# Attention with 8-wide heads: the band mask of the first layer added after the scores, in two 64x64 blocks instead of whole tiles

## The chip, the cores and the metric

The kernel is one program on one core of a Trainium2 chip. The metric is the device time of that program in microseconds (us), from launch to end. PE is TensorE (matmuls), PEld its weight loads, DVE VectorE, ACT ScalarE, POOL GpSimd.

## The reference

Four layers of cross attention and feed-forward on 32 sequences of 128 tokens with 128 features. The change touches only the first attention: 16 heads, each 8 wide, and a band mask that hides key k from query q where |q - k| is over 64.

```
q = _heads(query @ Wq.T + bq)
k = _heads(key @ Wk.T + bk)
v = _heads(value @ Wv.T + bv)
scores = jnp.einsum('bhqd,bhkd->bhqk', q, k) / np.sqrt(D_HEAD).astype(np.float32)
idx = jnp.arange(S)
local = jnp.abs(idx[:, None] - idx[None, :]) <= WINDOW // 2      # WINDOW = 128
scores = jnp.where(local[None, None, :, :], scores, -jnp.inf)
attn = jax.nn.softmax(scores, axis=-1)
```

With 128 queries and 128 keys, the mask hides something only where query and key lie in different halves of 64: in the two 64x64 blocks off the diagonal. In the two on the diagonal it is zero everywhere.

## The kernel before

`small_heads(l, phase)` computes this attention for layer 0 (and, with another mask, for layer 2). It handles one sequence per iteration, n = 0 to 31, in groups g of four (j = n % 4). Scores are computed twice. The first time they are written as queries x keys into `S` (the PSUM tile `pair`, two banks of 512 columns, so 8 heads at once: two passes p = 0 and 1 for the 16 heads); DVE takes the maximum over keys of each head (`maximum`, line 768). `split_max` (lines 776, 778) makes two bf16 parts of the negated maxima, and PE turns them over with one transpose (`turn_max`, line 582, into the PSUM tile `single`). The second time the scores are computed as keys x queries into `T` (the PSUM tile `quad`, four banks, all 16 heads: `turned`, line 598), the turned maxima are added to them (line 604), ACT takes the exponential (line 748), and `attend` (line 621) multiplies by the values and by ones. DVE divides (`normalise`, lines 784 and 786).

The mask is added by PE too. `mask_banks` (line 156) multiplies a 64x64 piece of an identity (bf16) by a broadcast of the mask: four matmuls of 64x64 by 512 columns fill two banks. They start the accumulation (`start=True`), and the scores are added on top. `S` takes four of them per pass (`mask_scores`), `T` takes eight (`mask_turned`).

There is one `S`, so pass 1 is written only after DVE has read pass 0, which `mask_scores` waits for (`s_free`). Each engine runs its instructions in the order of the code. On PE the order of iteration n is written out by hand:

```
(j==0: project_q, j==1: project_v, j==2: output, j==3: turn)   # "the head of the iteration"
mask_turned(n)
mask_scores(n + 2, 0)
turn_max(n + 1)
turned(n)
scores(n + 2, 0)
attend(n - 1)
(j==3: project_k)
mask_scores(n + 2, 1)
scores(n + 2, 1)
```

On DVE it is: other work of the group, `maximum(n+2, 0)`, `normalise(n-1)`, `maximum(n+2, 1)`, `split_max(n+2)`. Ahead of the loop a warm-up runs `mask_scores`, `scores` and `maximum` four times (m = 0, 1 and p = 0, 1), and `turn_max(0)`.

Of the kernel before, what the change touches and what calls it, by code (L numbers as in the profile page):

```python
# [20 lines left out]
P = 128  # L21
# [52 lines left out]
def program(nc, t, out):  # L74
    ctx = ExitStack()
    with ctx:
        def sb(name, shape, dtype=F32):
            return ctx.enter_context(nc.sbuf_tensor(name, shape, dtype))

        def sem(name):  # L80
# [8 lines left out]
        identb = sb("identb", [P, P], BF16)  # L89
# [3 lines left out]
        mask_bias = {l: {n: [sb(f"mask{n}{l}{half}", [P, P], BF16)[:] for half in ("own", "other")] for n in names}  # L93
                     for l, names in ((0, "S"), (2, "ST"), (3, "S"))}
# [56 lines left out]
        def mask_banks(pe, banks, masks):  # L151

            for r in range(2):
                rows = slice(64 * r, 64 * r + 64)
                for c in range(2):
                    pe.matmul(banks[r][64 * c:64 * c + 64, :], identb[rows, rows],
                              masks[r ^ c][rows, :].unsqueeze(1).broadcast_to([64, 4, P]), start=True, stop=False,
                              skip_group_check=True)

        def loop(eng, group, groups=NG, done=0):  # L160

            with eng.Fori(done // 2, groups // 2 - 1) as i:
                for u in range(2):
                    group(2 * i + u, u, False)
            for u in range(2):
                group(groups - 2 + u, u, u == 1)
# [253 lines left out]
        def small_heads(l, phase):  # L420
# [8 lines left out]
            qT = [arena.take([W]) for _ in range(2)]  # L429
# [20 lines left out]
            S, T, O, M = pair, quad, bank[6], bank[7]  # L450
# [9 lines left out]
            def strip(r):  # L460
                return slice(32 * r, 32 * r + 32)
# [27 lines left out]
            def tensor(pe):  # L489
# [68 lines left out]
                def mask_scores(m, p):  # L558

                    pe.wait_ge(s["s_free"], 2 * m + p)  # L560
                    mask_banks(pe, [S[:, r * 512:(r + 1) * 512] for r in range(2)], mask_bias[l]["S"])

                def scores(m, p):
                    g, j = divmod(m, G)
                    if j == 0 and p == 0:
                        pe.wait_ge(s["q_evac"], g + 1)
                        pe.wait_ge(s["kv_ready"], g + 1)
                    for r in range(2):
                        rows = strip(2 * p + r)
                        mm = pe.matmul(S[:, r * 512:(r + 1) * 512], qT[g % 2][rows, j * P:(j + 1) * P],  # L570
                                       kv[g % 2][rows, j, :, :].rearrange("p a k -> p (a k)"),
                                       start=False, stop=True, skip_group_check=True)
                    mm.then_inc(s["s_ready"], 1)

                def turn_max(m):
# [8 lines left out]
                def mask_turned(n):  # L584
                    if n == 0:
                        pe.wait_ge(s["k_evac"], 2)
                        pe.wait_ge(s["q_evac"], 1)
                        pe.wait_ge(s["v_evac"], 1)
                    pe.wait_ge(s["st_free"], 2 * n)
                    for r in (0, 2):  # L590
                        mask_banks(pe, [T[:, i * 512:(i + 1) * 512] for i in (r, r + 1)], mask_bias[l]["T"])

                def turned(n):

                    g, j = divmod(n, G)
                    for a in range(4):
                        for r in range(4):
                            pe.matmul(T[:, r * 512 + a * P:r * 512 + (a + 1) * P], kv[g % 2][strip(r), j, a, :],  # L598
                                      qT[g % 2][strip(r), j * P:(j + 1) * P], start=False, stop=False,
                                      skip_group_check=True)  # L600
                    pe.wait_ge(s["mts_ready"], n + 1)
                    for a in range(4):
                        for r in range(4):
                            mm = pe.matmul(T[:, r * 512 + a * P:r * 512 + (a + 1) * P], chooser[strip(r), a, :],  # L604
                                           mts[n % 2][strip(r), :], start=False, stop=True, skip_group_check=True)
                    mm.then_inc(s["st_ready"], 1)

                def attend(m):
# [24 lines left out]
                mm = pe.matmul(O[:, 0:P], vcol, wo[:], start=True, stop=True)  # L633
                if l == 2:
                    pe.wait_ge(s["tables_ready"], 1)
                    pe.wait_ge(s["c_squared"], 1)
                    mm = pe.matmul(lg_part[:, 0:E], ones, cT2, start=True, stop=True)
# [8 lines left out]
                for m in range(2):  # L646
                    for p in range(2):
                        mask_scores(m, p)
                        scores(m, p)
                pe.wait_ge(s["cvec_ready"], 1)  # L650
                turn_max(0)
                for n in range(N):
                    g, j = divmod(n, G)
                    if j == 0 and routes(g):
                        turn_rows(g - 2)
                    if j == 0 and g + 1 < NG and l == 0:
                        project_q(g + 1, M)
                    elif j == 1 and g + 1 < NG:
                        project_v(g + 1, M)
                    elif j == 2 and g >= 1:  # L660
                        output(g - 1)
                    elif j == 3 and g + 2 < NG:
                        turn(g + 2)
                    mask_turned(n)
                    if n + 2 < N:
                        mask_scores(n + 2, 0)
                    if n + 1 < N:
                        turn_max(n + 1)
                    if j == 0 and g + 1 < NG and l == 2:
                        project_q(g + 1, M)  # L670
                    turned(n)
                    if n + 2 < N:
                        scores(n + 2, 0)
                    if n >= 1:
                        attend(n - 1)
                    if j == 3 and g + 2 < NG:
                        project_k(g + 2, M)
                    if n + 2 < N:
                        mask_scores(n + 2, 1)
                        scores(n + 2, 1)  # L680
# [1670 lines left out]
        def wide_heads(phase):  # L2351
# [131 lines left out]
            def tensor(pe):  # L2483
# [23 lines left out]
                def scores(t):  # L2507

                    g, j, o = t // 8, t // 2 % G, t % 2
                    if t % 8 == 0:  # L2510
                        ring_copied(pe, ("q", g, HB - 1))
                        ring_copied(pe, ("k", g, HB - 1))
                    if t >= 2:
                        pe.wait_ge(s["exp_done"], t - 1)
                    mask_banks(pe, [S[o][:, r * 512:(r + 1) * 512] for r in range(2)], mask_bias[3]["S"])
                    for i in range(4):
                        for r in range(2):
                            rows = slice(64 * r, 64 * r + 64)
                            mm = pe.matmul(S[o][:, r * 512 + i * P:r * 512 + (i + 1) * P],  # L2519
                                           qT[g % 2][rows, 4 * o + i, j * P:(j + 1) * P],  # L2520
                                           kT[g % 2][rows, 4 * o + i, j * P:(j + 1) * P],
                                           start=False, stop=(i == 3), skip_group_check=True)
                    mm.then_inc(s["s_ready"], 1)
# [365 lines left out]
```

## Time and profile before

| | before |
|---|---|
| device time, median of 3 runs | 2033.67 us (2032.84 to 2035.79) |
| span of the profiled execution, first to last instruction | 2027.5 us |
| first-layer attention loop within it | about 36.9 to 280 us |
| PE busy over the whole span | 1766.7 us (87%) |
| DVE busy over the whole span | 1092.1 us (54%) |
| ACT busy over the whole span | 891.5 us (44%) |

For the profiled execution the profile gives its span; its time with launch and end is not listed apart. The median of the runs is 6.2 us above the span, and that difference is taken as the work around the span. A row of the timeline gives the start in us from the span's start and the length. Matmuls overlap: the end of a PE row is modelled and lies behind the start of the next, so what PE really spends is read from start to start. The `f32` matmuls show twice as many instances in the trace as in the code, since each runs as two passes.

### The profile page before, as it was taken

How to read it: one execution, taken by the hardware profiler on the slowest of the kernel's cores; microseconds unless marked ns; L12 is line 12 of the kernel's file. 1: busy time of each engine (PE TensorE's matmuls, PEld its weight loads, DVE VectorE, ACT ScalarE, POOL GpSimd, SP SyncE). 2: the span in 40 equal slices, each digit the busy share in tenths (PEclk: the TensorE clock that was granted, in tenths of full speed). 3: DMA queues.
4: the chain of work that ended last, by engine and by line, in shares of the span. 5: the costliest groups of instructions: out<-in, count | busy, mean ns of one | idle time of the engine just before them, and what ended most of it. 6: DMA issues, size and time to landing. Idle time of an engine off the chain costs nothing.

```text
span 2027.5 us, 48497 instructions
## 1 busy us (share of the span) xinstructions
PE 1766.7 (87%) x18886; PEld 1258.1 (62%) x18886; DVE 1092.1 (54%) x3147; ACT 891.5 (44%) x2432; POOL 652.9 (32%) x656
## 2 busy tenths in 40 slices
PE   6999985587869999998999971999699999999978
PEld 3565564576648778873565551999456666666753
DVE  4666657567532222214566763656465656665548
ACT  2333320476334444432333320666265555556525
POOL 3233201467311111103214426455133233333405
PEclk8999996788679999997999995999799999999969
DMA  5000000000000000007210001222200000000001
GB/s 174 7 13 8 2 2 9 28 16 1 1 6 1 1 2 2 1 1 293 104 76 18 18 18 45 61 57 58 90 17 17 17 17 17 6 1 1 1 1 42
DMA packets 48828, 63.55 MB, mean 31 GB/s; under 512 B 8106, under 2 KB 37701, under 8 KB 48349
## 3 DMA queue, kind: packets, MB, share of 16 engines
q1 hardware_dynamic: 44253, 51.98, 7.8%
q0 software_dynamic: 4352, 8.47, 1.3%
q8 instruction: 156, 2.56, 0.5%
q14 instruction: 67, 0.55, 0.1%
HBM read 32.29 MB, written 28.65 MB: 30 GB/s over the span
## 4 chain that ended last, share of the span: by engine, by line
PE 57%; DVE 9%; issue 7%; POOL 4%; POOLq 3%; DVEq 2%; ACT 1%; DMA 1%; SPq 1%; PEldq 0%; PEld 0%; ACTq 0%
PE single L1835 5%; PE quad L1823 5%; PE pair L570 3%; PE single L621 3%; PE single L2156 3%; PE quad L2139 2%; PE quad L2145 2%; PE pair L1796 2%; PE quad L598 2%; PE pair L2519 2%; POOL tokens_by_expert L417 2%; DVE arena L768 1%; PE quad L2554 1%; PE quad L2545 1%; PE single L2531 1%
## 5 line engine op out<-in xcount | busy, mean ns | idle before, releaser
L768 DVE TENSOR_REDUCE arena<-pair 128x8 f32<-128x1024 f32 x128 | 156.7, 1224 | 140.4 <-PE pair L570 138.4
L2757 POOL TENSOR_TENSOR arena<-arena 128x512 f32<-128x512 f32 x128 | 130.4, 1040 | 296.2 <-DVE arena L2676 296.2
L263 POOL TENSOR_TENSOR rstd<-var_eps,neg_half 128x4 f32<-128x4 f32 (+1 forms) x64 | 65.5, 1024 | 350.3 <-DVE var_eps L259 266.7
L748 ACT ACTIVATE arena<-quad 128x1024 f32<-128x1024 f32 x128 | 124.1, 1021 | 69.3 <-PE quad L604 65.0
L1908 ACT ACTIVATE arena<-quad,arena 128x256 f32<-128x256 f32 x256 | 110.7, 475 | 98.1 <-PE quad L1823 98.1
L892 POOL TENSOR_SCALAR arena<-arena 128x512 f32<-128x512 f32 x56 | 86.7, 1565 | 196.6 <-ACT arena L690 196.5
L570 PE MATMUL pair<-arena 32*128 32x512 f32 x512 | 147.3, 652 | 0.0
L1999 DVE TENSOR_TENSOR arena<-single,arena 128x512 f32<-128x512 f32 x32 | 22.1, 692 | 206.2 <-PE single L1835 206.2
L2612 ACT ACTIVATE arena<-pair,arena 128x128 f32<-128x128 f32 x256 | 90.9, 381 | 89.0 <-DVE arena L2671 89.0
L2612 ACT ACTIVATE arena<-quad,arena 128x128 f32<-128x128 f32 x256 | 90.9, 381 | 86.4 <-DVE arena L2671 86.4
L1835 PE MATMUL single<-wide,arena 128*64 128x128 f32 x2048 | 123.9, 275 | 0.0
L1823 PE MATMUL quad<-arena,wide 128*128 128x256 f32 x512 | 121.6, 385 | 2.6 <-issue 1.8
L1835 PEld LDWEIGHTS single<-wide,arena 128*64 128x64 f32 x2048 | 110.7, 137 | 15.7 <-issue 10.0
L1823 PEld LDWEIGHTS quad<-arena,wide 128*128 128x128 f32 x512 | 93.2, 190 | 18.5 <-issue 6.4
L2336 POOL DMA_INDIRECT outputs_by_choice<-arena x72 | 71.0, 986 | 88.3 <-DVE arena L2289 72.9
L2280 DVE SCALAR_TENSOR_TENSOR arena<-quad,arena 114x128 f32<-114x128 f32 x216 | 62.4, 344 | 48.6 <-ACT arena L2190 25.1
L2190 ACT ACTIVATE arena<-quad,arena 114x128 f32<-114x128 f32 x216 | 63.5, 365 | 55.9 <-PE quad L2139 46.8
L784 DVE RECIPROCAL arena<-single 128x128 f32<-128x128 f32 x64 | 61.2, 957 | 47.8 <-PE single L621 37.3
L417 POOL DMA_INDIRECT tokens_by_expert<-arena x64 | 62.8, 981 | 74.8 <-PE single L621 37.8
L717 ACT ACTIVATE arena<-single 128x128 bf16<-128x128 bf16 x64 | 17.7, 277 | 151.4 <-PE single L582 151.0
L621 PEld LDWEIGHTS single<-arena 128*32 128x32 f32 x2048 | 52.3, 109 | 49.2 <-issue 48.8
L2033 POOL TENSOR_TENSOR arena<-arena 128x512 f32<-128x512 f32 x32 | 34.8, 1096 | 134.2 <-DVE arena L1978 134.2
(502 smaller groups left out, 4376.7 us busy)
## 6 DMA issues: line engine op xcount, KB each, us to landing
tokens_by_expert<-arena SPq DMA_DIRECT2D x22, 780.0 KB, 8.6
arena<-in_ctxT SPq DMA_DIRECT2D x32, 256.0 KB, 3.0
arena<-tokens_by_expert SPq DMA_DIRECT2D x72, 65.0 KB, 1.8
wide<-in_w SPq DMA_DIRECT2D x2, 2048.0 KB, 10.1
arena<-outputs_by_choice SPq DMA_DIRECT2D x16, 256.0 KB, 4.1
wide<-in_wgu SPq DMA_DIRECT2D x1, 2736.0 KB
x<-in_x SPq DMA_DIRECT2D x4, 512.0 KB, 7.9
out_x<-x SPq DMA_DIRECT2D x8, 256.0 KB, 2.3
```

The lines of the kernel that those rows point to most:

```text
L417: pool.indirect_dma_start(by_tile, bass.IndirectOffsetOnAxis(ap=where_i[:, i, n:n + 1], axis=0), xr[:, n, :], None).then_inc(routed, 16)
L570: mm = pe.matmul(S[:, r * 512:(r + 1) * 512], qT[g % 2][rows, j * P:(j + 1) * P], kv[g % 2][rows, j, :, :].rearrange("p a k -> p (a k)"), ...
L621: mm = pe.matmul(O[strip(c), k * P:(k + 1) * P], lhs(h), probs[m % 2][:, h, :], start=(a == 0), stop=(a == 3), skip_group_check=True)
L748: act.activation(probs[n % 2][:, 8 * p:8 * p + 8, :].rearrange("p h q -> p (h q)"), T[:, 1024 * p:1024 * p + 1024], ACT.Exp).then_inc(s["s ...
L768: dve.tensor_reduce(mx[m % 2][:, 8 * p:8 * p + 8], S[:].rearrange("p (h k) -> p h k", h=8), AX.X, ALU.max).then_inc(s["s_free"], 1)
L892: mm = pool.tensor_scalar(kv[g % 2][:, :, a, :], kf[g % 2], kmask[:, a:a + 1], None, ALU.mult)
L1823: pe.matmul(bank[2 + f][:, 0:G * K], w1[:, e, f * P:(f + 1) * P], exT[u][:, e, :], start=True, stop=True).then_inc(s["h_ready"], 1)
L1835: mm = pe.matmul(bank[6 + pair % 2][K * r:K * r + K, j * P:(j + 1) * P], h1T[e % 4][:, f, j * K:(j + 1) * K], w2[:, e, f, :], start=(f == ...
L1908: act.activation(h1T[e % 4][:, f, :], bank[2 + f][:, 0:G * K], ACT.Gelu_apprx_tanh, bias=b1c[:, e, f:f + 1]).then_inc(s["h_evac"], 1)
L2336: pool.indirect_dma_start(done, bass.IndirectOffsetOnAxis(ap=back_i[:, n:n + 1], axis=0), ysb[n % SLOTS], None, bounds_check=2 * B * P - 1 ...
L2612: mm = act.activation(probs[t % 3][:, i, :], S[t % 2][:, i * P:(i + 1) * P], ACT.Exp, bias=minus_max[t % 3][:, i:i + 1], accum_out=total[t ...
L2757: pool.tensor_tensor(part, part, inv[t % 3][:, 4 * r:4 * r + 4].unsqueeze(2).broadcast_to([P, 4, P]), ALU.mult).then_inc(s["norm_ready"], 1)
```

## The change

In layer 0 alone, `mask_banks` is not called any more. A new helper, `mask_across`, adds the mask only where it is not zero: each of its four matmuls writes 4 x 64 columns (in each of the four heads of a bank, the half of the columns that lies off the diagonal) instead of 512. It runs after the scores, as the end of the accumulation: behind the two score matmuls of each pass into `S`, and behind the added maxima in `T`. The first score matmul of each bank now starts the accumulation. The semaphores that tell DVE (`s_ready`) and ACT (`st_ready`) that a tile is ready are raised by the last mask matmul. The waits for a free tile stay where they were. Layer 2 keeps the code of before.

```diff
+        def mask_across(pe, banks, masks):
+
+            for r in range(2):
+                rows = slice(64 * r, 64 * r + 64)
+                for c in range(2):
+                    far = slice(64 - 64 * c, 128 - 64 * c)
+                    mm = pe.matmul(banks[r].rearrange("p (a k) -> p a k", a=4)[64 * c:64 * c + 64, :, far],
+                                   identb[rows, rows], masks[r ^ c][rows, far].unsqueeze(1).broadcast_to([64, 4, 64]),
+                                   start=False, stop=True, skip_group_check=True)
+            return mm
...
                 def mask_scores(m, p):
 
                     pe.wait_ge(s["s_free"], 2 * m + p)
-                    mask_banks(pe, [S[:, r * 512:(r + 1) * 512] for r in range(2)], mask_bias[l]["S"])
+                    if l == 2:
+                        mask_banks(pe, [S[:, r * 512:(r + 1) * 512] for r in range(2)], mask_bias[l]["S"])
...
-                                       start=False, stop=True, skip_group_check=True)
+                                       start=(l == 0), stop=True, skip_group_check=True)
+                    if l == 0:
+                        mm = mask_across(pe, [S[:, r * 512:(r + 1) * 512] for r in range(2)], mask_bias[l]["S"])
                     mm.then_inc(s["s_ready"], 1)
...
                     pe.wait_ge(s["st_free"], 2 * n)
-                    for r in (0, 2):
-                        mask_banks(pe, [T[:, i * 512:(i + 1) * 512] for i in (r, r + 1)], mask_bias[l]["T"])
+                    if l == 2:
+                        for r in (0, 2):
+                            mask_banks(pe, [T[:, i * 512:(i + 1) * 512] for i in (r, r + 1)], mask_bias[l]["T"])
...
-                                      qT[g % 2][strip(r), j * P:(j + 1) * P], start=False, stop=False,
+                                      qT[g % 2][strip(r), j * P:(j + 1) * P], start=(l == 0 and a == 0), stop=False,
...
+                    if l == 0:
+                        for r in (0, 2):
+                            mm = mask_across(pe, [T[:, i * 512:(i + 1) * 512] for i in (r, r + 1)], mask_bias[l]["T"])
                     mm.then_inc(s["st_ready"], 1)
```

Lines move by 11 to 18 with it: 570 becomes 582, 582 becomes 596, 598 and 604 become 613 and 619, 621 becomes 639, and the mask matmuls of layer 0 are at line 166. Two places on PE show what moves. The first is the middle of a loop iteration. Before, from the added maxima (line 604) over pass 0 of the scores (570) and `attend` (621) to pass 1 of the scores:

```order
L604 MATMUL quad<-arena 128x128 x16
L570 MATMUL pair<-arena 128x512 x2
L621 MATMUL single<-arena 32x128 x16
L621 MATMUL single<-arena,ones_cols 32x128 x16
L156 MATMUL pair<-maskS0own,identb 64x512
L156 MATMUL pair<-maskS0other,identb 64x512 x2
L156 MATMUL pair<-maskS0own,identb 64x512
L570 MATMUL pair<-arena 128x512 x2
```

And now, from the added maxima (619) over pass 0 of the scores (582) to `attend` (639):

```order
L619 MATMUL quad<-arena 128x128 x16
L166 MATMUL quad<-maskS0own,identb 64x4x64
L166 MATMUL quad<-maskS0other,identb 64x4x64 x2
L166 MATMUL quad<-maskS0own,identb 64x4x64 x2
L166 MATMUL quad<-maskS0other,identb 64x4x64 x2
L166 MATMUL quad<-maskS0own,identb 64x4x64
L582 MATMUL pair<-arena 128x512 x2
L166 MATMUL pair<-maskS0own,identb 64x4x64
L166 MATMUL pair<-maskS0other,identb 64x4x64 x2
L166 MATMUL pair<-maskS0own,identb 64x4x64
L639 MATMUL single<-arena 32x128 x16
L639 MATMUL single<-arena,ones_cols 32x128 x16
```

Twelve mask matmuls of half the columns have come in between the added maxima and `attend`; the four full ones between `attend` and pass 1 of the scores are gone.

The second place is the end of an iteration and the head of the next: from pass 1 of the scores over the transposes of `turn` to `turn_max`. Before:

```order
L570 MATMUL pair<-arena 128x512 x2
L520 MATMUL single<-ident,arena 128x128 x4
L156 MATMUL quad<-maskS0own,identb 64x512
L156 MATMUL quad<-maskS0other,identb 64x512 x2
L156 MATMUL quad<-maskS0own,identb 64x512 x2
L156 MATMUL quad<-maskS0other,identb 64x512 x2
L156 MATMUL quad<-maskS0own,identb 64x512
L156 MATMUL pair<-maskS0own,identb 64x512
L156 MATMUL pair<-maskS0other,identb 64x512 x2
L156 MATMUL pair<-maskS0own,identb 64x512
L582 MATMUL single<-identb,arena 128x128
```

And now:

```order
L582 MATMUL pair<-arena 128x512 x2
L166 MATMUL pair<-maskS0own,identb 64x4x64
L166 MATMUL pair<-maskS0other,identb 64x4x64 x2
L166 MATMUL pair<-maskS0own,identb 64x4x64
L531 MATMUL single<-ident,arena 128x128 x4
L596 MATMUL single<-identb,arena 128x128
```

The twelve full mask matmuls ahead of `turn_max` are gone; four half ones stand behind pass 1 of the scores.

## Rows read from the trace of the kernel before

**Rows 1.** Two stretches: PE, PEld, DVE, ACT, POOL busy; granted clock; DMA share; GB/s.
```profile
21.50:36.90 15.40, 11.35 (x37) 2.82 (x35) 5.60 (x8) 1.36 (x3) 5.33 (x4) 0.60 0.87 337
36.90:280.00 243.10, 234.04 (x4412) 140.90 (x4415) 153.67 (x346) 86.01 (x120) 58.98 (x52) 1.00 0.03 8
```

**Rows 2.** Line 582, the turn of the maxima, in its 32 instances of the first layer.
```profile
L582 PE MATMUL single<-identb,arena x32: 229/229/286, 35.0 to 273.8; 128*128 128x128 bf16 x32
...
  DVE arena L778: 16.7, 38
```

**Rows 3.** Timeline of one iteration: start us, length us, engine, line, operation, tiles, count, idle before.
```profile
204.30 0.10 PEld L582 LDWEIGHTS single<-identb,arena 128*128 128x128 bf16 x1 [0.41 <-DVE arena L778]
...
205.46 0.40 PE L604 MATMUL quad<-arena 32*128 32x128 bf16 x16
...
205.69 1.08 PE L570 MATMUL pair<-arena 32*128 32x512 f32 x4
...
206.69 1.08 PE L621 MATMUL single<-arena 128*32 128x128 f32 x32
206.81 1.22 DVE L768 TENSOR_REDUCE arena<-pair 128x8 f32<-128x1024 f32 x1 [1.51 <-PE pair L570]
...
207.59 1.06 PE L621 MATMUL single<-arena,ones_cols 128*32 128x128 f32 x32
...
208.58 0.40 PE L156 MATMUL pair<-maskS0own,identb 64*64 64x512 bf16 x1
...
208.72 0.96 DVE L784 RECIPROCAL arena<-single 128x128 f32<-128x128 f32 x1 [0.68 <-PE single L621]
...
208.92 1.13 PE L570 MATMUL pair<-arena 32*128 32x512 f32 x4
209.75 0.29 DVE L786 TENSOR_TENSOR arena<-single,arena 128x128 f32<-128x128 f32 x1
...
209.98 1.16 PE L555 MATMUL single<-wo,arena 128*128 128x128 f32 x8
210.09 1.23 DVE L768 TENSOR_REDUCE arena<-pair 128x8 f32<-128x1024 f32 x1
...
211.06 0.40 PE L156 MATMUL quad<-maskS0own,identb 64*64 64x512 bf16 x1
...
211.10 0.11 PEld L156 LDWEIGHTS quad<-maskS0own,identb 64*64 64x64 bf16 x1
211.31 0.38 PE L156 MATMUL quad<-maskS0other,identb 64*64 64x512 bf16 x2
...
211.52 0.38 PE L156 MATMUL pair<-maskS0other,identb 64*64 64x512 bf16 x2
...
211.66 0.18 DVE L778 SCALAR_TENSOR_TENSOR arena<-arena 128x16 bf16<-128x16 f32 x1
211.77 0.69 DVE L812 TENSOR_TENSOR x<-single,arena 128x512 f32<-128x512 f32 x1
211.89 0.10 PEld L582 LDWEIGHTS single<-identb,arena 128*128 128x128 bf16 x1 [0.41 <-DVE arena L778]
```

**Rows 4.** Timeline, an iteration that has no projection, transpose or output at its head.
```profile
265.69 0.40 PE L156 MATMUL pair<-maskS0own,identb 64*64 64x512 bf16 x1 [0.77 <-DVE arena L768]
```

**Rows 5.** Timeline, an iteration with a key projection ahead of its second pair of scores.
```profile
226.33 1.23 DVE L768 TENSOR_REDUCE arena<-pair 128x8 f32<-128x1024 f32 x1 [1.11 <-PE pair L570]
```

**Rows 6.** Timeline of the warm-up ahead of the loop, and the loop's first turn.
```profile
28.43 0.63 PE L156 MATMUL pair<-maskS0own,identb 64*64 64x512 bf16 x1 [1.33 <-DVE arena L768]
...
29.00 2.08 PE L570 MATMUL pair<-arena 32*128 32x512 f32 x4
...
35.06 2.02 PE L537 MATMUL single<-arena,wq 128*128 128x512 f32 x2
...
36.66 0.18 DVE L778 SCALAR_TENSOR_TENSOR arena<-arena 128x16 bf16<-128x16 f32 x1
...
38.35 0.23 PE L582 MATMUL single<-identb,arena 128*128 128x128 bf16 x1
```

## Prediction

> **What bounds the kernel now.** I looked first at the granted clock and at busy time in the stretch that the change touches. The loop of the first layer takes 243.1 us at full clock (1.00, the level of 2.4 GHz) with PE busy for 234.0 of them [rows 1]. That looks like a PE-bound loop, in which narrower mask matmuls must pay. The second view, who waits for whom, says otherwise: the turn of the maxima (line 582) waits for DVE's line 778, 16.7 us in all over its 32 instances [rows 2]. So the third view was the timeline of one iteration, to see what PE's work lies beside.
>
> An iteration is 7.59 us, from turn to turn (204.30 to 211.89) [rows 3]. From the turn to the end of `attend` PE runs without a pause: doubled scores, added maxima (205.46), pass 0 of the scores (205.69), `attend` (206.69 to 208.65). Then come the old masks of pass 1 (208.58) and pass 1 of the scores (208.92, ending 210.05). With that DVE starts its second maximum at 210.09 and line 778 ends at 211.84; PE turns at 211.89. These 1.8 us on DVE are fixed, and PE fills them with the head of the iteration (209.98) and with twelve mask matmuls (211.06, 211.31, 211.52), and still sits idle for 0.41 us before the turn. Where there is no head work PE is idle 0.77 us even before those masks [rows 4]. The loop is thus a ring: PE from the turn to the scores of pass 1, DVE from there to the next turn. What PE does inside DVE's part is free; what it does in its own part counts in full.
>
> **What the change does to the ring.** It takes the twelve masks out of DVE's part. That gains nothing: the turn waits for line 778 as before, and the idle time grows. It puts twelve half masks on PE's own part, and four more behind pass 1 of the scores, where DVE waits for them. Only the four old masks ahead of pass 1 come off the ring.
>
> Prices, from starts in [rows 3]. A round of four mask matmuls (they run side by side, one row stands for them) of 512 columns takes 0.25 us (211.06 to 211.31) or 0.21 (to 211.52). The trace shows no round of 256 columns; I take half, 0.12 and 0.11, as the columns are what streams. If the narrow, strided form gained nothing it would stay 0.25 and 0.21. Between matmuls that use the array in different pieces there is a gap: old masks of pass 1 to scores 0.34 us, less a round of 0.21, is 0.13. From `attend` to the masks: its last half has 8 groups that start 0.11 apart from 207.59, so it would be through at 208.49, and the masks start at 208.58, 0.09 later. I take 0.09 to 0.13 for a gap, between rows of different kinds: 0.12 on average. Scores right behind masks also last 1.13 us instead of the 1.08 behind line 604: 0.05 more.
>
> - Masks of `T` between line 604 and pass 0: gap 0.12, rounds 0.12 and 0.11, gap 0.12, and 0.05 on the scores: +0.52.
> - Masks of pass 0 between scores and `attend`: the gap that is there now stays, one round and one more gap: +0.21.
> - Pass 1: the masks ahead go, -0.34. Those behind start where PE's next work starts now, 1.06 after the scores (208.92 to 209.98), and last 0.40 less half a round, 0.29. DVE can start at 1.35 instead of 1.13: +0.22. Sum -0.12.
>
> Does DVE take up that -0.12? Its own chain after `attend` is the reciprocal (208.72) and line 786, which ends 210.04. DVE starts an operation up to 0.07 before the shown end of the one before (line 778 ends 211.84, line 812 starts 211.77), so the maximum could start at 209.97, 0.12 earlier than now. It fits exactly; I take -0.12, with 0 as the other end. Where a key projection delays pass 1, DVE waits 1.11 us for the scores [rows 5], and the -0.12 counts surely.
>
> An iteration gets 0.52 + 0.21 - 0.12 = 0.61 us longer. There are 30 turn-to-turn stretches from the loop's first turn at 38.35 to the last at 273.8 [rows 2, 6]: +18.3 us. The exponential on ACT, one iteration ahead of its reader, and DVE's first maximum (which waits 1.51 us now, 206.81) move along with PE and cost nothing more. The last two iterations have masks of `T` on the path but lose some ahead of it: an estimate of +0.3.
>
> **The warm-up gains.** There the clock is 0.60 on average [rows 1], mostly at the lower level of 1.2 GHz, and DVE and PE take turns. The masks ahead take 0.57 us off (28.43 to 29.00), those behind give back some 0.3: about -0.9 over four passes. The loop's first turn at 38.35 comes 1.5 us behind DVE's line 778 (36.66 to 36.84), because a projection (35.06, 2.02 us) and twelve slow masks stand ahead [rows 6]. Without the masks it can come when the projection ends, which starts some 0.8 us earlier than now: near 36.3, 2.05 earlier. But the clock rises only near 38, so some 1.6 us of the following work runs at half speed, losing 0.8. Warm-up: -1.25.
>
> **Sum.** 18.3 + 0.3 - 1.25 = 17.4 us. The profiled span of 2027.5 becomes 2044.9; with 6.2 us around it, as the median of before has, 2051.1. Layer 2 and all else are unchanged.
>
> **A rule weighed.** In [rows 3] the weight load of the second round of masks stands at 211.10, while the first round, on the same rows of the array, still streams until 211.31. The Trainium skill ("TensorE: Matmul & The Clock Gate", Part 3, The mechanism) says that a weight load overlaps matmuls in flight only where its row group differs. By that rule, the second round of `T` would wait for its load. The trace speaks against it here; as a mechanism of this kernel it is rival 3.
>
> **Rivals.**
> 1. *PE's columns bound the loop, and it gets faster.* Four rounds an iteration shrink by 0.21 to 0.25 each to half: -0.46 us, times 31 is -14 us, 2019. For it: PE busy 234 of 243 us. It decides only if PE reaches the turn after DVE's line 778 even without masks. With masks it is there 0.41 us early, in [rows 4] more. 4 in 100.
> 2. *The inserted masks hide in the array's gaps*, at under 0.15 us an iteration: within 4 us of before, 2034 to 2038. Nothing shows matmuls of different pieces overlapping; the gaps of 0.09 to 0.13 speak against it. 4 in 100.
> 3. *The second narrow round waits for its weights*, a load of 0.11 [rows 3]: +0.11 for `T` in 30 iterations, 3.3 us more, 2054. A narrow round has less streaming to cover a load than a wide one has. 12 in 100; it lies inside the range.
> 4. *Narrowing gains nothing*: rounds stay 0.25 and 0.21. `T` 0.75, pass 0 0.33, pass 1 about 0: +1.08, times 30, less 1, is 31 us: 2065. 8 in 100.
> 5. *The longer pauses of PE let the clock fall.* PE's idle time before the turn grows from 0.4 to about 1 us. The loop stands at 1.00 through pauses of 0.77 [rows 4]. Were a tenth of it at half speed, 24 us more: 2075. 3 in 100.
>
> The forecast itself has 69 in 100. Its low end: gaps of 0.09, rounds of 0.105, no 0.05: `T` 0.39, pass 0 0.20, pass 1 -0.12: 0.47, times 30 is 14.1, and a warm-up of -2.5: 2045.5. Its high end, gaps of 0.13 and no gain in pass 1, is 0.75 times 30 and 0: 2056. With rival 3 that is 81 in 100; 2045 to 2059 takes in all of it and a little of rival 4.
>
> A change of under 0.2% (4 us) can't be told from none here. Faster: rival 1, 4 in 100. Same: most of rival 2, 3. Slower: all else, 93.
>
> **What would show it.** In the profile after: turns 8.2 us apart where they were 7.59; line 582 of before (now 596) waiting about 1 us for DVE in most iterations; the doubled scores to `attend` stretch 0.7 longer; DVE's wait before the first maximum longer by as much; PE busy a smaller share of a longer loop; the first loop turn near 36.3. I am wrong if PE no longer waits before the turn, if narrow rounds start 0.2 us apart, or if the clock drops below 1.00 inside the loop.

## The result

The changed kernel takes 2071.91 us (median of 4 runs, 2063.08 to 2075.42) where the kernel before took 2033.26. The ratio is 1.0189, with an interval of 1.0163 to 1.0215: slower, as forecast, but by 39 us instead of 17, and outside the range of 2045 to 2059. The profiled execution has a span of 2061.5 us, 34.0 more than before. It was the fastest of the four runs (2063.08); the other three took 7 to 12 us longer, and no trace shows in what.

The first view again is busy time and granted clock, in three stretches: from the loop's first turn of the maxima to its last (33.09 to 306.77), and two single iterations. Columns as in [rows 1].

```profile
33.09:306.77 273.68, 235.96 (x4207) 147.76 (x4207) 149.44 (x334) 82.98 (x116) 58.58 (x51) 0.93 0.03 10
119.83:129.71 9.88, 8.96 (x145) 6.14 (x146) 5.05 (x11) 2.21 (x3) 0.62 (x1) 0.83 0.06 21
129.71:138.07 8.36, 6.94 (x141) 4.39 (x142) 5.40 (x13) 2.81 (x4) 0.00 (x0) 1.00 0.01 3
```

The loop, turn to turn, takes 273.7 us; before it was 235.5 (38.35 to 273.80). PE is busy for 236 us of it: no longer nearly all. And the clock is not 1.00 any more, but 0.93 on average. The two single iterations (second and third row) are both without a key projection: at full clock (the level of 2.4 GHz) one takes 8.36 us, with the clock at 0.83 (partly at 1.2 GHz) the other takes 9.88.

The turn of the maxima, now line 596, waits for DVE far longer than before:

```profile
L596 PE MATMUL single<-identb,arena x32: 216/216/289, 31.0 to 306.8; 128*128 128x128 bf16 x32
...
  issue: 49.6, 34
  DVE arena L786: 34.0, 27
```

These 34.0 us are all idle time of PE's matmuls (the same view of PE alone gives the same row); the weight loads stand under "issue". The 16.7 us of [rows 2] are for the greater part idle time of the weight loads, 14.4 us. For PE's matmuls alone, line 582 before has

```profile
  DVE arena L778: 2.3, 8
```

so PE's own recorded pauses ahead of the turn went from 2.3 to 34.0 us.

The third view is one iteration at full clock. It is of the kind of [rows 3], with the value projection in the place of the output projection at its end:

```profile
217.27 0.10 PEld L596 LDWEIGHTS single<-identb,arena 128*128 128x128 bf16 x1 [2.00 <-issue]
...
218.44 0.40 PE L619 MATMUL quad<-arena 32*128 32x128 bf16 x16
...
218.77 0.29 PE L166 MATMUL quad<-maskS0own,identb 64*64 64x256 bf16 x1
...
218.91 0.27 PE L166 MATMUL quad<-maskS0other,identb 64*64 64x256 bf16 x2
...
219.12 1.13 PE L582 MATMUL pair<-arena 32*128 32x512 f32 x4
...
220.17 0.29 PE L166 MATMUL pair<-maskS0own,identb 64*64 64x256 bf16 x1
...
220.41 1.08 PE L639 MATMUL single<-arena 128*32 128x128 f32 x32
...
222.29 1.13 PE L582 MATMUL pair<-arena 32*128 32x512 f32 x4
...
223.35 0.29 PE L166 MATMUL pair<-maskS0own,identb 64*64 64x256 bf16 x1
...
223.46 0.29 DVE L804 TENSOR_TENSOR arena<-single,arena 128x128 f32<-128x128 f32 x1
...
223.71 1.23 DVE L786 TENSOR_REDUCE arena<-pair 128x8 f32<-128x1024 f32 x1
...
225.28 0.18 DVE L796 SCALAR_TENSOR_TENSOR arena<-arena 128x16 bf16<-128x16 f32 x1
...
225.63 0.10 PEld L596 LDWEIGHTS single<-identb,arena 128*128 128x128 bf16 x1 [1.08 <-issue]
```

From turn to turn it is 8.36 us (217.27 to 225.63), 0.77 more than the 7.59 of [rows 3]. Piece by piece, start to start:

| piece of the ring | before | after | difference | forecast |
|---|---|---|---|---|
| turn to line 604 / 619 | 1.16 | 1.17 | +0.01 | 0 |
| 604 / 619 to pass 0 of the scores, over the masks of `T` | 0.23 | 0.68 | +0.45 | +0.47 |
| pass 0 of the scores to `attend`, over its masks | 1.00 | 1.29 | +0.29 | +0.26 |
| `attend` to DVE's second maximum | 3.40 | 3.30 | -0.10 | -0.12 |
| DVE's second maximum to the turn | 1.80 | 1.92 | +0.12 | 0 |

(The forecast's 0.05 on the scores behind masks is counted in the third line here.) The narrow rounds start 0.14 us apart (218.77 and 218.91), the gaps that are left between starts less a round of 0.11 are 0.10 to 0.13, and DVE takes up the 0.10 that pass 1 loses. One line was not foreseen: the turn starts 0.18 us after the end of DVE's last operation (225.28 + 0.18 to 225.63), where it was 0.05 before.

The two traces differ by 34.0 us of span. The loop's first turn comes 5.3 us earlier (33.09 for 38.35). From the first turn to the last it is 38.2 us more. What follows the last turn has 1.1 us more.

```profile
17.78 0.60 PE L531 MATMUL single<-ident,arena 128*128 128x128 f32 x4
...
19.79 1.23 DVE L786 TENSOR_REDUCE arena<-pair 128x8 f32<-128x1024 f32 x1 [2.11 <-PE pair L166]
...
33.09 0.26 PE L596 MATMUL single<-identb,arena 128*128 128x128 bf16 x1
```

The first maximum starts at 19.79 us; before, it started at 23.20. The last work ahead of the first scores and masks, the transposes of line 531 (520 before), starts at 17.78; before:

```profile
21.02 0.66 PE L520 MATMUL single<-ident,arena 128*128 128x128 f32 x4
```

So 3.2 of the 5.3 us were won ahead of anything that the change touches. In that execution PE had the full clock from 14.2 to 21.0 us, in the one of before from 21.1 to 24.6; over the fourteen traces of this study the first maximum starts anywhere from 19.79 to 23.20. The stretch from those transposes to the loop's first turn, which the change does touch, shrank from 17.33 to 15.31 us, 2.0.

### The profile page after: what moved, and what is told of

The parts are those of the page before. It is cut to its first block, busy times and chain, and to the rows that moved or that the text cites. A ratio compares the mean times of both kernels' runs of the same rounds, so it can differ in the third digit from the quotient of the medians.

```text
span 2061.5 us, 48527 instructions
## 1 busy us (share of the span) xinstructions
PE 1768.5 (86%) x18886; PEld 1268.5 (62%) x18886; DVE 1093.7 (53%) x3147; ACT 891.0 (43%) x2432; POOL 653.3 (32%) x656
## 4 chain that ended last, share of the span: by engine, by line
PE 56%; issue 9%; DVE 9%; POOLq 3%; POOL 3%; DVEq 2%; ACT 1%; DMA 1%; SPq 1%; PEldq 0%; PEld 0%; ACTq 0%
PE single L1853 5%; PE quad L1841 5%; PE pair L582 3%; PE single L639 3%; PE quad L2157 2%; PE single L2174 2%; PE quad L2163 2%; PE quad L613 2%; PE pair L1814 2%; PE pair L2537 2%; DVE arena L786 1%; PE quad L2572 1%; PE quad L2563 1%; PE single L2549 1%; PE single L2521 1%
## 5 line engine op out<-in xcount | busy, mean ns | idle before, releaser
L582 PE MATMUL pair<-arena 32*128 32x512 f32 x512 | 152.4, 673 | 5.4 <-DVE arena L786 5.4
L428 POOL DMA_INDIRECT tokens_by_expert<-arena x64 | 62.8, 981 | 75.2 <-PE single L639 38.2
L613 PE MATMUL quad<-arena 32*128 32x128 f32 x2048 | 82.7, 303 | 0.2 <-ACT arena L766 0.2
```

## The experiments

The kernel before does not take the same time on every chip: 2033 us in the measurement above, 2014 to 2027 in the groups below. The only trace of it is the one of the first chip. The one other kernel that was traced on two chips and held its clock (experiment 4) has 7.48 us an iteration on both, and loops of 231.9 and 232.2 us; what follows the last turn took 1739.5 us on one and 1756.9 on the other. So ratios and the rows of the loop are compared, not times across groups.

**1. Filler where the masks were** (e1_cover). It tells the cost of the longer ring from that of the clock.

```diff
                     pe.wait_ge(s["s_free"], 2 * m + p)
-                    if l == 2:
+                    if l == 2 or p == 0:
                         mask_banks(pe, [S[:, r * 512:(r + 1) * 512] for r in range(2)], mask_bias[l]["S"])
...
-                    if l == 2:
+                    if True:
                         for r in (0, 2):
                             mask_banks(pe, [T[:, i * 512:(i + 1) * 512] for i in (r, r + 1)], mask_bias[l]["T"])
```

> The changed kernel with the old wide masks put back as a mere filler where they stood: eight into T and four into pass 0 of S in DVE's part of the ring, overwritten by the scores, which still start the accumulation; the narrow masks behind stay. Theory 'ring plus clock': of the 34 us of span that the changed kernel lost, some 15 came from stretches at 1.2 GHz that followed from PE's pauses, some 24 from longer iterations (0.77 each), with 5 gained ahead of the loop. With the filler PE is busy again in DVE's part, so the clock stays at 1.00 throughout the loop; the turn's waits are as before too, so iterations last 7.59 + 0.65 = 8.24 us. Total about 2033 + 19 to 21 = 2053. Rival 'only the ring': the clock fell by chance of phase and not for the pauses; then some stretches at 1.2 GHz remain, and the time is 2060 to 2072. Rival 'columns': PE streams more than before in every iteration, so it would be the slowest of all, over 2075.

Measured: ratio 1.0125 (1.0109 to 1.0140), 2039.05 against 2014.28. The loop's row:

```profile
35.63:295.74 260.11, 250.40 (x4567) 148.25 (x4563) 148.16 (x326) 82.56 (x115) 58.59 (x51) 0.98 0.03 8
```

Iterations take 8.22 us, as expected; the total is 25 us above before, where 19 to 21 were expected. The clock is 0.98 over the loop, not quite 1.00: it fell near the loop's start and once among the last iterations, which have no head work and pauses of 0.90 us in spite of the filler. PE issues 12 more mask matmuls an iteration than the changed kernel, and the kernel is faster. That is against any theory by which PE's columns matter here, and for "ring plus clock".

**2. The waits behind the turn** (e2_waits).

```diff
-                    pe.wait_ge(s["s_free"], 2 * m + p)
                     if l == 2:
+                        pe.wait_ge(s["s_free"], 2 * m + p)
...
+                    if l == 0:
+                        pe.wait_ge(s["s_free"], 2 * m + p)
                     for r in range(2):
...
-                    pe.wait_ge(s["st_free"], 2 * n)
                     if l == 2:
+                        pe.wait_ge(s["st_free"], 2 * n)
...
+                    if l == 0:
+                        pe.wait_ge(s["st_free"], 2 * n)
                     for a in range(4):
```

The new places in layer 0 are ahead of the matmuls of `scores` and of `turned`; the waits ahead of the masks are kept for layer 2 alone.

> The changed kernel with the two waits for free tiles (s_free, st_free) moved from ahead of the turn of the maxima to the first matmul that writes the tile, behind it. In the changed kernel the turn starts 0.18 us after the end of DVE's last operation, before the change it was 0.05. Theory: with no mask matmul to carry them, those two waits pile up on the turn, and the sequencer works through what is left of them after the maxima are ready. Then the distance returns to 0.05 and an iteration at full clock lasts 8.23 instead of 8.36 us, about 4 us in all. Rival: the 0.18 is the price of restarting PE after a pause of a microsecond; then nothing changes, 8.36. The total moves with the clock as well (the changed kernel's runs were 2063 to 2075) and is expected at 2058 to 2071.

Ratio 1.0160 (1.0144 to 1.0176). The timeline around a turn (line 800 is DVE's last operation of `split_max`, line 598 the turn):

```profile
203.60 0.18 DVE L800 SCALAR_TENSOR_TENSOR arena<-arena 128x16 bf16<-128x16 f32 x1
203.83 0.10 PEld L598 LDWEIGHTS single<-identb,arena 128*128 128x128 bf16 x1 [1.50 <-DVE arena L800]
```

The turn starts 0.05 us after DVE's end (203.78 to 203.83) although PE had paused for over a microsecond: the 0.18 was no price of a restart. In the changed kernel five waits stand ahead of the transpose, where before there were three, and the one for the maxima is no longer the last. The records of PE's sequencer in the trace of the changed kernel show it at the turn of 225.63: a first record, with the wait for the maxima and one other, ends at 225.50, 0.04 us behind DVE's end (225.46); a second one, with two more waits, stands from 225.56 to 225.61; the fifth wait is on the weight load itself, at 225.63. Before, the record with the two other waits was through at 211.43, and the load carried the wait for the maxima. Moving two waits takes 0.13 us off that distance, and iterations take 8.22 us. The clock fell as much as in the changed kernel (0.94 over the loop).

**3. The narrowing without the move** (e3_narrow_ahead): `mask_across` with `start=True`, called where `mask_banks` was, and the scores added on top as before.

> The kernel before with the masks where they were, ahead of the scores, but in the narrow form (only the two blocks off the diagonal, starting the accumulation): the narrowing without the move. Ring theory: only the round ahead of pass 1 is on the ring; it shrinks from 0.21 to 0.11 us, DVE can take up 0.1, so iterations last 7.48 to 7.49 us instead of 7.59: -3 us over 30. PE's pauses ahead of the turn grow by 0.34 us to 0.5 to 1.1. If the clock holds, 2030; if such pauses make it fall, up to 2045. Columns theory: four rounds at half width save 0.46 us an iteration, 14 us in all: 2019.

Ratio 1.0024 (1.0006 to 1.0041). Two successive turns, then the loop's row:

```profile
204.03 0.23 PE L592 MATMUL single<-identb,arena 128*128 128x128 bf16 x1 [0.22 <-DVE arena L788]
...
211.51 0.23 PE L592 MATMUL single<-identb,arena 128*128 128x128 bf16 x1 [0.22 <-DVE arena L788]
```

```profile
34.07:277.55 243.48, 227.73 (x4207) 143.41 (x4203) 149.01 (x331) 82.55 (x116) 58.47 (x51) 0.95 0.03 10
```

The ring did what was expected, 7.48 us from turn to turn, and it brought no gain: the clock is 0.95 over the loop. It fell in its first iterations and twice among the last four, where PE pauses for 0.98 us for want of head work. The columns theory, 14 us faster, is refuted.

**4. Narrow only where it is on the ring** (e5_pass1_narrow; e11_pass1_again is the same kernel in a later group). `mask_scores` calls the narrow form for layer 0 and p = 1, else `mask_banks`.

> The kernel before with the narrow mask for pass 1 of S alone, ahead of its scores; T and pass 0 keep the wide masks, which lie in DVE's part and cover PE's pause there. Ring theory: 0.10 us an iteration saved, 7.49 instead of 7.59, with the clock held at 1.00: about -3 us, 2030. If DVE can't start its maximum earlier because its own chain after attend ends at the same time, 0 to -1 us. Columns theory: one round of four, -3.5 us.

> The variant with pass 1's mask narrow and ahead once more, to see whether its 0.11 us an iteration, read from the trace, can be told in the time: ring theory 0.9985 to 0.999 (-3 us in the loop), and an interval with the first group's that lies below 1. Rival: the loop gains 3 us but what follows gives it back, 1.000.

Ratios 0.9989 (0.9976 to 1.0002) and 0.9988 (0.9978 to 0.9999).

```profile
201.22 0.23 PE L592 MATMUL single<-identb,arena 128*128 128x128 bf16 x1
...
208.70 0.23 PE L592 MATMUL single<-identb,arena 128*128 128x128 bf16 x1
```

```profile
37.99:269.85 231.86, 223.39 (x4206) 135.48 (x4203) 148.33 (x326) 82.50 (x115) 58.43 (x51) 1.00 0.03 8
```

7.48 us again, with the clock at 1.00 through the loop in both: the wide masks of `T` and pass 0, which cost nothing where they stand, keep PE busy. But the six iterations with a key projection take 8.78 us as before. There the narrow mask's 0.10 is lost again on DVE, whose first part of `split_max` takes 0.42 us instead of 0.32, beside a long operation of POOL. Before, and here (line 786, the line 776 of before):

```profile
227.65 0.32 DVE L776 TENSOR_SCALAR arena<-arena 128x16 bf16<-128x16 f32 x1
...
193.01 0.42 DVE L786 TENSOR_SCALAR arena<-arena 128x16 bf16<-128x16 f32 x1
```

So the ring gives 24 times 0.11 us, 2.6 us or 0.9987, and both intervals hold it; the first interval alone does not exclude no gain at all.

**5. The changed kernel again** (e8_after_again), on one chip with e4, e6 and e7 below.

> The changed kernel once more, as the partner of this group. On the chip of the first group the kernel before took 2014.3 us instead of 2033.3, with the same 7.59 us an iteration in its loop, so only ratios and loop rows are compared across groups. Theory: iterations at full clock 8.36 us again, several at the lower clock, at other places than in the first trace; ratio to before 1.015 to 1.022. Rival: the clock's falls were a property of the first chip or run; then the loop stays at 1.00 and the ratio is about 1.010.

Ratio 1.0190 (1.0173 to 1.0207), the same as on the first chip.

```profile
33.73:314.99 281.26, 243.53 (x4207) 152.49 (x4207) 149.37 (x334) 82.97 (x116) 58.58 (x51) 0.91 0.03 9
```

8.36 us at full clock, and the clock is 0.91 over this loop, lower than in the first trace (0.93), with 9 falls instead of 7, in part in the same iterations and in part in others. The loops of the two traces of one kernel differ by 7.6 us (281.3 and 273.7); the runs of this group scatter by 3.5 us, those of the first by 12.

**6. The move without the narrowing** (e4_wide_behind): 4 x 128 columns in the new helper.

> The changed kernel with masks of full width (512 columns a matmul) in the new places: the move without the narrowing. If a narrow round really costs half, each of the four rounds is 0.10 us longer and all lie on the ring: 8.36 + 0.42 = 8.78 us an iteration. If the narrow strided form streams no faster, 8.36. The clock may hold better, as PE has more to do, but the pauses ahead of the turn are as long as in the changed kernel. Ratio to before 1.024 to 1.035.

Ratio 1.0238 (1.0221 to 1.0255), where 1.024 to 1.035 was expected.

```profile
33.97:318.89 284.92, 247.52 (x4206) 146.00 (x4207) 149.38 (x334) 83.10 (x116) 58.61 (x51) 0.94 0.03 9
```

Iterations take 8.79 us at full clock, 0.43 more than with narrow masks: each of the four rounds really costs half when narrow, and each counts in full. The narrowing was worth 0.43 us an iteration in the new place, and 0.11 in the old.

**7. No mask at all, and no mask with filler** (e6_no_mask, e10_no_mask_cover). The first leaves out the mask of layer 0, with the waits as in 2. The second issues the wide masks of `T` and pass 0 and overwrites them, so that no mask takes effect either.

> The variant with the waits behind the turn, with the mask of layer 0 left out altogether (its output is computed without the band). It has PE's long pauses ahead of the turn but nothing on the ring that the kernel before lacks. Ring theory: only pass 1's masks come off the ring and DVE's own chain allows 0.11 us of that: 7.47 us an iteration at full clock. Clock theory: pauses of 0.9 us and more make the clock fall even so, and the time is 2 to 12 us above what the ring gives; ratio to before 0.998 to 1.005. If pauses don't matter: the loop at 1.00 and a ratio of 0.997 or less. Columns theory: 16 rounds-of-four fewer columns, 0.9 us an iteration, ratio 0.986.

> No mask takes effect in layer 0 (its output is computed without the band), but the wide masks of T and of pass 0 are still issued in DVE's part as filler and then overwritten. Against the run without any mask it has the same ring and differs only in that PE is busy ahead of the turn. Clock theory: the clock stays at 1.00 in most of the loop, iterations last 7.47 us, and the ratio to before is 0.997 to 1.000, where the run without masks had 1.008. Rival: that run was slow for another reason, and the filler, being more work, makes it slower still, over 1.01.

Without masks the ratio is 1.0084 (1.0067 to 1.0101), above even the 0.998 to 1.005 expected with a falling clock: less work than the kernel before, and slower. Its turns, and its loop:

```profile
211.66 0.23 PE L596 MATMUL single<-identb,arena 128*128 128x128 bf16 x1 [0.95 <-DVE arena L795]
...
219.10 0.23 PE L596 MATMUL single<-identb,arena 128*128 128x128 bf16 x1 [0.95 <-DVE arena L795]
...
226.54 0.23 PE L596 MATMUL single<-identb,arena 128*128 128x128 bf16 x1 [1.46 <-DVE arena L795]
...
238.33 0.23 PE L596 MATMUL single<-identb,arena 128*128 128x128 bf16 x1 [1.04 <-DVE arena L795]
```

```profile
32.05:290.95 258.90, 221.90 (x3726) 144.04 (x3727) 149.21 (x334) 82.98 (x116) 58.52 (x51) 0.87 0.04 13
```

At full clock 7.44 us, shorter than before. But behind every fourth iteration, whose pause is 1.46 us, the next takes 11.79 instead of 8.78 (226.54 to 238.33): the clock has fallen. It is 0.87 over the loop. With the filler put back the ratio is 0.9988 (0.9970 to 1.0006), and the loop:

```profile
34.18:267.52 233.34, 221.33 (x4087) 135.03 (x4083) 147.77 (x326) 82.52 (x115) 58.54 (x51) 0.98 0.04 11
```

The same turn distance (7.45 us, 205.22 to 212.67; with a key projection 8.55 instead of 8.78), more matmuls, and 25.6 us less in the loop (233.3 for 258.9). The programs of this pair differ in filler and in where two waits stand alone; the two ran on different chips, and each is compared with the kernel before on its own. So the clock's loss comes from PE standing idle in DVE's part. No run here separates the length of a pause from the amount of work around it.

**8. Half of the change** (e7_T_behind): `T` as in the changed kernel, `S` as before.

> Half of the change: the masks of T narrow and behind the scores as in the changed kernel, those of S wide and ahead as before. From the rows of the changed kernel T's masks cost 0.50 us on the ring (two rounds 0.24, two gaps 0.21, 0.05 on the scores behind): 8.09 us an iteration, 15 us in all. S's masks still carry the wait for their tile, so the turn starts 0.05 us after DVE again. PE's pause ahead of the turn is about 0.7 us, between those of before and of the changed kernel; the clock falls in fewer iterations or not at all. Ratio to before 1.007 to 1.012.

Ratio 1.0100 (1.0082 to 1.0119).

```profile
34.48:295.79 261.31, 240.16 (x4206) 145.93 (x4203) 149.61 (x332) 82.73 (x116) 58.57 (x51) 0.95 0.03 9
```

8.09 us between turns, as forecast to the hundredth. PE's waits ahead of a turn add up to 0.35 to 0.85 us in most of the loop, and there the clock held; it fell in the first iterations and in the last, behind pauses of 1.33 and 1.42.

**9. Scores where PE waits** (e9_scores_first): from the ring. Pass 0 of the scores is issued ahead of the turn, in DVE's part, and `S` has narrow masks.

```diff
                         mask_scores(n + 2, 0)
+                        if l == 0:
+                            scores(n + 2, 0)
...
-                    if n + 2 < N:
+                    if n + 2 < N and l == 2:
                         scores(n + 2, 0)
```

> A version meant to beat both, from the ring: T's masks wide and ahead as before; the masks of S narrow and ahead; and pass 0 of the scores moved ahead of the turn, where PE only waits for DVE. From DVE's second maximum the ring then runs over mask and scores of pass 0 (0.05 + 0.23 + 1.06), the turn and the doubled scores (1.4), to attend, in place of split (0.52 + 0.05), turn and doubled scores (1.4) and scores (1.0): 0.22 us an iteration less, and with the 0.11 of pass 1's narrow mask 7.25 us instead of 7.59. PE has no pause left, so the clock stays at 1.00. 30 times 0.34 is 10 us: ratio 0.995. Rival: DVE's other work (residuals, statistics) now delays the first maximum or the turn, and the iterations that have it stay at 7.5: ratio 0.998 to 1.000.

Ratio 0.9964 (0.9951 to 0.9977), 2019.25 against 2026.97: faster than both kernels.

```profile
202.42 1.23 DVE L780 TENSOR_REDUCE arena<-pair 128x8 f32<-128x1024 f32 x1
...
203.63 0.38 PE L156 MATMUL quad<-maskS0other,identb 64*64 64x512 bf16 x2
...
203.84 0.27 PE L166 MATMUL pair<-maskS0own,identb 64*64 64x256 bf16 x1
...
203.98 0.18 DVE L790 SCALAR_TENSOR_TENSOR arena<-arena 128x16 bf16<-128x16 f32 x1
...
204.05 1.13 PE L580 MATMUL pair<-arena 32*128 32x512 f32 x4
...
205.11 0.23 PE L592 MATMUL single<-identb,arena 128*128 128x128 bf16 x1
...
205.66 1.21 DVE L780 TENSOR_REDUCE arena<-pair 128x8 f32<-128x1024 f32 x1
...
212.46 0.23 PE L592 MATMUL single<-identb,arena 128*128 128x128 bf16 x1
```

From turn to turn 7.35 us here (205.11 to 212.46) and in seven others, 7.47 in twelve, 8.50 in the six with a key projection. The turn no longer waits for DVE: line 790 ended at 204.16, and the turn at 205.11 follows the scores. I had forecast 7.25: in that order PE hardly pauses in most iterations, so the wide masks of `T` are on the path, free before: DVE frees `S` at 203.65, and the mask of pass 0 starts at 203.84, behind them.

**10. And `T` narrow too** (e12_all_narrow).

> The variant with pass 0 of the scores ahead of the turn, whose iterations last 7.47 us where the head has work for PE and 7.35 us where it has none, and in which PE never waits in the former; now T's masks are narrow and ahead too. There the ring runs over PE alone, so T's masks, free in the kernel before, lie on it: two rounds shrink by 0.23 us, until PE waits for DVE's second maximum (s_free) again, as in the iterations without a head. So 7.35 us in all but the project_k iterations (8.50 to 8.3): 0.12 to 0.2 us in some 26 iterations, 3 to 4 us. With pauses of about 0.1 to 0.2 us the clock holds. Ratio to before 0.994 to 0.9955. Rival: T's masks are still covered, 7.47 stays, 0.9964.

Ratio 0.9988 (0.9971 to 1.0005).

```profile
36.16:266.71 230.55, 223.82 (x4200) 140.98 (x4199) 146.72 (x324) 82.52 (x115) 57.66 (x51) 0.97 0.03 8
```

The iterations did shrink to 7.35 us, but the loop as a whole took 230.6 us, not less than the 229.5 of e9: the clock is 0.97 over it, against 0.99. It fell near the start and once among the last iterations, behind pauses of 0.98 us; e9, whose pauses there are 0.77, fell near the start alone. The runs scatter by 15 us. So the expected 3 to 4 us were not had. Version 9 has the lowest ratio measured; its interval and this one just overlap.

## Why the prediction was right and where it was wrong

**Right: the ring.** PE's work inside DVE's part is free, and outside it counts in full. Experiments 3, 4, 6 and 8 each changed a part of the terms, and the turn distances without a key projection came out as the ring says, within 0.02 us. Forecast and measured terms for the masks of `T` and of pass 0 are 0.73 and 0.74 us, for pass 1 -0.12 and -0.10. Rivals 1 (columns) and 2 (hidden masks) fall with the same runs. Rival 3 falls too: a second narrow round started 0.14 us behind the first, less than a load of 0.11 and the streaming of 0.11 in turn would need. There the rule in the Trainium skill ("TensorE: Matmul & The Clock Gate", Part 3, The mechanism) that a weight load overlaps matmuls in flight only where its row group differs would have added 0.1 us, and the rows do not show it; the same section also lets a load go ahead into a background weight buffer, which would agree with the rows. Rival 4 falls with experiment 6.

Three readings of the prediction were off without harm to the ring. The 0.41 us of [rows 3] is the idle time of the weight loads; the last wide round starts at 211.52 and takes 0.21, so the matmuls pause for some 0.16 us before the turn at 211.89. The 16.7 us of [rows 2] mix both in the same way. And "the -0.12 counts surely" where a key projection stands does not hold: in experiment 4 those iterations stayed at 8.78 us.

**Wrong, the step that failed most: "The loop stands at 1.00 through pauses of 0.77".** The forecast put the clock's loss at nothing. I gave the falling clock 3 in 100, because the trace of before held the clock through 0.77 us at the end of the loop. But the change made such pauses longer (0.92, 1.2 and 1.42 us in turn, 2.0 at the end) and put one into every iteration. Had every turn distance been that of full clock (24 of 0.77 more and 6 with a key projection of 0.88 more, 23.8 us), the loop would have grown by 23.8 us. It grew by 38.2. The other 14.4 us are the iterations at the lower clock. The pair in experiment 7 shows the cause, experiments 1 and 3 agree. Rival 5 had the right mechanism and, at 24 us on top of the forecast, a size of the same order; its chance of 3 in 100 was wrong.

**Mis-sized: the iteration, 0.61 forecast, 0.77 measured.** Of the 0.16, 0.13 is the turn's start: two waits that mask matmuls used to carry came to stand on the turn. Experiment 2 shows it. I had looked at what the removed matmuls did, not at which waits they carried. In iterations with a key projection another 0.1 comes from DVE, whose line 794 took 0.42 us beside POOL's long operation, where line 776 had taken 0.32. In all 23.8 us instead of 18.3. One sum was off as well: by the prediction's own prices the term of pass 0, one round (0.11 or 0.12) and one gap (0.12), is 0.23 or 0.24, not 0.21. With the 0.05 on the scores that makes 0.28 to 0.29, and 0.29 was measured.

**Mis-sized: the warm-up, -1.25 forecast, -5.3 in the trace.** The part that the change touches gave 2.0; the other 3.2 lie ahead of the first scores and masks, where the two programs are the same, and are a difference between executions. That was luck, and in this trace it hid 3.2 us of the miss.

Sum: -5.3 + 23.8 + 14.4 + 1.1 = 34.0 us, the difference of the spans (the 1.1 us behind the last turn were forecast as 0.3). It accounts for the profiled execution; the median is 8.8 us above it, and the clock's falls there are not on record. What stays open: why one pause is followed by a fall and the next, as long, is not. In the changed kernel's first trace the clock fell behind three of the seven pauses of about 1.4 to 1.5 us and held behind the other four, in the kernel without masks it fell behind five of the six of 1.46. No run here tells what decides between them.

## What to carry to other kernels

Before work is taken off an engine or moved, find the ring that sets an iteration, and ask of each piece whether it lies in the part where that engine waits anyway: there it is free, even useful as cover for the TensorE clock, and narrowing it can cost time. What filled such a pause best here was work of the ring itself, as pass 0 of the scores in experiment 9; the masks were only harmless filler. And a removed instruction leaves its waits behind: look at which instruction they land on, and whether it then still waits for the critical semaphore last.

## What the runs showed that I had not expected

A kernel with the masks left out was slower than with them: 1.0084, its loop 258.9 us against 233.3 with dead matmuls as filler. In the fourteen traces of this study the granted clock fell to its level of 1.2 GHz 54 times between the loop's first and last turn, each time within a pause of PE or up to 1.5 us behind its end: all but two of those pauses were of 0.96 to 2.04 us, the two of 0.90 (e1) and 0.77 (e9). There were 7 and 9 falls in the two traces of the changed kernel, 9 without masks, 7, 6, 5 and 4 in e4, e2, e7 and e3, 2 in each of e1, e10 and e12, 1 in e9, and none in the kernel before, e5 and e11. And the 0.92 us pauses of the changed kernel, its most frequent, were never followed by a fall. The loop of before has a pause of 1.33 us, in its first iteration, and one of 1.09 (108.57 to 109.66), and kept 1.00 all the same; so did the loops of e5 and e11 with one of 1.33 each. So the length of a pause alone does not decide. The same kernel before took 2033 us on one chip and 2014 us on another, while the changed kernel's ratio was the same on two chips, 1.0189 and 1.0190.
